# Key matmul before V's in the woven projections, and the norm of the attention's output in two parts

## The chip, the cores and the metric

The program runs on 8 cores of one Trainium2 chip (cores 0 to 3 on one die, 4 to 7 on the other) with no exchange between them. Each core has five engines with a queue of its own: TensorE (PE; weight loads stand as PEld), VectorE (DVE), ScalarE (ACT), GpSimd (POOL) and SyncE (SP), which here only issues DMAs. An engine works through its queue in order and stops where it waits for a semaphore. The metric is the device time of the slowest core, in us, as the median of several runs.

## The reference, cut to what matters

Each core has one batch element b = core // 2 and every second block of 128 of its rows: 2048 tokens of its own, and keys and values of all 4096. Sizes: D 1024, 16 heads, a latent of 128, 32 channels a head for scores, 32 for values, and an FFN of 4096 inner channels.

```python
q = rms_norm((x @ Wq).reshape(b, t, 16, 64).transpose(0, 2, 1, 3))
kv = x @ Wkv                                  # t x 128
k = rms_norm((kv @ Wk)...)                    # 16 heads x 32
v = (kv @ Wv)...                              # 16 heads x 32
probs = softmax(causal(q[..., :32] @ k.T / 8))
x1 = layernorm(x + pad(probs @ v) @ Wo)       # post-norm
gate, up = silu(bitlinear(x1, w_gate)), bitlinear(x1, w_up)
y = layernorm(x1 + bitlinear(gate * up, w_down))
# bitlinear: activations scaled by the row's maximum to -128..127 and rounded,
# weights scaled by their mean absolute value and rounded to -1, 0, 1
```

## The kernel before

The program is recorded once: helpers `pe`, `act`, `dve`, `pool` and `dma` append an instruction to an engine's queue, with the semaphore values (cT, cA, cV, cG for TensorE, ScalarE, VectorE, GpSimd) that it waits for. So the order in a queue is the order in which the Python code runs, and that is woven from generators: whoever calls `next` on one of them appends its next piece.

**Attention** (`attention`, L810). The core's 2048 queries are four groups `tc` of 512; in each, four groups `gi` of four heads; in each, the key blocks `sc` of 128 (8 tc + 8 of them): 320 steps. One step puts four score matmuls (L827) into four PSUM banks, two exponentials of 128x1024 on ScalarE (L840), a mask on GpSimd for diagonal blocks (L848 or L853), and, two steps late (LAG 2), the sums of probabilities into `ps_den` (L782) and the products with V into `ps_pv` (L793). After the last block of a group of heads `chain` (L763) empties both banks and divides, on VectorE (L771 to L776). After a `tc` its four tiles of 128 rows are appended to `wo_pend`, the list of pieces of `wo_ln1`.

**Pieces woven into the steps.** (1) While there are any left, one stage of `projections` (L617) follows each step. (2) From the fourth block of a group of heads on, `wo_step(2)` takes two pieces of `wo_pend`, unless the FFN is in its down projection. (3) Pieces of the weight stream (`stream_step`): per FFN weight block an absolute sum (DVE L366 or ScalarE), or two casts (DVE L382 and L385, 1.3 to 1.4 us each), with loads and stores. (4) Once projections and stream are done, the FFN (`ffn`, L1161) is woven in at a fixed rate: `up` (matmuls L986; ScalarE L999; VectorE L1005, L1017, L1022), quantization of the hidden rows (GpSimd L1058, VectorE L1061, a DMA transpose), `down` (L1109), and its own norm. A unit u is two tiles (2u, 2u+1); `down` first waits, by its yields, until `wo_pend` is empty (or the attention is over).

**Projections.** Chunks of 512 tokens, c5 = 2 to 7 in this woven part: for even c5 four jobs `queries2` (three stages), for each c5 four jobs `keys_values2` (two stages and a last piece), and `latent2` (L528), 8 matmuls in two halves, which makes the latent of the next chunk, second to last of the jobs of each. A key/value job (L563) makes V (matmul L567, VectorE's copy into `vtok` L571), the keys (matmul L575), their squares (ScalarE L432), in the next stage `inv_rms` (matmul L441 with ones, ScalarE Ln L448 and Exp L451), and at its end VectorE's product `khat` (L582). All of it shares two PSUM banks, `ps_w0` and `ps_w1`, from a ring `wring` that hands out the bank that was given back first:

```python
b3 = wring.take()          # V's bank: matmul L567, copy L571, then given back
b1 = wring.take()          # key's bank: matmul L575, held until khat (L582)
```

The loop around the jobs keeps one job `old` whose last piece is outstanding:

```python
for _ in range(stages):
    next(job)
    if old is not None:
        next(old, None)
        old = None
    yield
old = job
```

**Norm of the attention's output** (`wo_ln1`, L704). For tile `ti` (buffer `r_t[ti % 2]`, named r_t or S in the trace): `project(0)` and `project(1)` (four matmuls with Wo each, L714, and VectorE's add of x, L719), `norm1` (`layernorm_stats`: two bn_stats L690 and bn_aggr L692 on VectorE, then two tiny operations on GpSimd, L693 and L696, the second of which makes the power -0.5; then VectorE's normalization L727 of 128x1024), `quant` (VectorE L731, L733, L734, L735, L736, L738), and `store` (two stores and the load of x of tile ti + 2; it also sets `ln_done`, on which the FFN's `try_prologue` goes). `store` has an empty piece ahead of it, so a tile is six pieces, three steps. Two places finish `wo_pend` at once: `chain` of the next `tc`'s first group of heads (gi == 0), and the end of the attention. `factors` (L939, VectorE L942 to L946) needs `swb`, the mean of the FFN's weights (L336).

## Time and profile before

| | us |
|---|---|
| runs of the kernel before: median of 3 (each) | 1638.44 (1638.44, 1637.69, 1682.19) |
| the profiled execution, its own time | 1643.48 |
| its span on the slowest core (6); the other cores | 1641.9; 1625.1 to 1640.1 |
| mean granted TensorE clock, share of 2.4 GHz | 0.851 to 0.858 over the cores |
| busy on that core: TensorE, VectorE, ScalarE, GpSimd | 1302.4, 806.2, 824.7, 317.9 |

By stretches of the slowest core (busy us and granted clock):

| us | what runs | TensorE | DVE | ACT | clock |
|---|---|---|---|---|---|
| 0 to 90 | first projections, loads of x and weights | 34.9 | 23.4 | 37.6 | 0.80 |
| 90 to 205 | attention tc 0 (to 218), woven projections | 80.5 | 72.6 | 78.5 | 0.70 |
| 205 to 300 | tc 1 (218 to 475), projections, norms of tiles 0 to 3 | 62.0 | 56.6 | 55.7 | 0.71 |
| 300 to 455 | tc 1, projections | 120.3 | 88.9 | 120.7 | 0.50 and 0.69 |
| 455 to 560 | tc 2, norms of tiles 4 to 7, the FFN starts | 74.5 | 67.8 | 67.0 | 0.69 |
| 560 to 1190 | tc 2 and 3 with FFN woven in | 547.0 | 263.1 | 421.3 | 0.94 |
| 1190 to 1642 | norms of tiles 12 to 15, rest of the FFN | 383.3 | 233.8 | 44.0 | 0.93 |

How to read it: no engine is busy throughout, TensorE comes nearest; what each stretch is worth is told by the waits in it. In a timeline a row is start, duration, engine, line, operation, out<-in with shapes, and in brackets how long the engine had been idle before it and for whom. "x4" counts instructions that the row puts together.

### The profile page before, as it was taken

What the parts mean: (1) busy time and instruction counts of PE and PEld (TensorE: products, weight loads), DVE (VectorE), ACT (ScalarE), POOL (GpSimd) and SP (SyncE); (2) the same over time, 40 slices, a digit from 0 to 9 for tenths busy, and PEclk for the clock granted to TensorE, in tenths of its full rate; (3) what the DMA queues carried; (4) which work ended last, traced back from release to release, by engine and by line L of the source; (5) the groups of instructions that cost most, each with busy time, mean ns of one, the idle gap of its engine ahead of it and who ended that gap; (6) DMA issues with size and microseconds to landing.
All of it is one profiled execution on the core that took longest, in us unless ns stands there. A gap on an engine that the chain in (4) does not pass through costs nothing.

```text
span 1641.9 us, 22928 instructions; the slowest of 8 cores (1625.1 to 1641.9 us)
## 1 busy us (share of the span) xinstructions
PE 1302.4 (79%) x7494; PEld 438.3 (27%) x7494; DVE 806.2 (49%) x1158; ACT 824.7 (50%) x998; POOL 317.9 (19%) x350
## 2 busy tenths in 40 slices
PE   1676675788666888979869898989868999898966
PEld 0221121122111222222212222222223444343422
DVE  2227875468447766143561434143347762635522
ACT  2577564878784676657546686768601210111100
POOL 1024412033020304121123003130220020202021
PEclk8876686567556998989979998999989999898978
DMA  9995765779595785523255232523165585765646
GB/s 249 275 274 168 224 213 192 172 250 276 188 272 191 259 231 157 130 80 101 85 159 130 90 91 73 159 81 105 60 179 197 176 209 189 169 206 155 187 138 159
DMA packets 146514, 283.07 MB, mean 172 GB/s; under 512 B 91744, under 2 KB 92000, under 8 KB 133088
## 3 DMA queue, kind: packets, MB, share of 16 engines
q1 hardware_dynamic: 144816, 272.70, 54.6%
q0 software_dynamic: 1584, 8.91, 3.5%
q8 instruction: 64, 1.05, 0.3%
q14 instruction: 50, 0.41, 0.1%
HBM read 235.96 MB, written 33.55 MB: 164 GB/s over the span
## 4 chain that ended last, share of the span: by engine, by line
PE 51%; DVE 18%; issue 11%; ACT 8%; DMA 7%; POOL 3%; SPq 1%; DVEq 1%; ACTq 0%; POOLq 0%
PE ps_w L986 14%; PE ps_w L1109 6%; PE ps_sc L827 6%; ACT PT L840 5%; PE ps_den L782 4%; PE ps_sc L986 4%; PE ps_pv L793 3%; PE ps_sc L1109 3%; DVE S L775 3%; DMA R<-scr_w 2%; PE ps_w L547 2%; DVE st L690 2%; DMA R<-R 2%; DVE qb L382 2%; PE ps_w L714 2%
## 5 line engine op out<-in xcount | busy, mean ns | idle before, releaser
L840 ACT ACTIVATE PT<-ps_sc,negM 128x1024 bf16<-128x1024 f32 (+3 forms) x640 | 592.7, 983 | 197.6 <-PE ps_sc L827 195.3
L986 PE MATMUL ps_w<-R,S 128*128 128x512 fp8e4 x1280 | 336.1, 393 | 34.0 <-DVE R L1005 20.3
L827 PE MATMUL ps_sc<-qn,khat 32*128 32x512 bf16 (+3 forms) x1280 | 200.4, 397 | 63.5 <-ACT PT L840 58.7
L848 POOL TENSOR_TENSOR PT<-PT,tri 128x512 bf16<-128x512 bf16 x64 | 80.3, 1254 | 530.4 <-ACT PT L840 528.7
L986 PEld LDWEIGHTS ps_w<-R,S 128*128 128x128 bf16 x1280 | 106.4, 99 | 210.2 <-issue 121.0
L782 PE MATMUL ps_den<-PT,ones 128*32 128x512 bf16 (+3 forms) x1280 | 131.7, 402 | 18.4 <-DVE S L771 10.3
L853 POOL TENSOR_SCALAR PT<-PT,hflag_sb 128x512 bf16<-128x512 bf16 x64 | 112.9, 1763 | 111.0 <-ACT PT L840 110.9
L793 PE MATMUL ps_pv<-PT,vtok 128*32 128x512 bf16 (+3 forms) x1280 | 130.6, 398 | 0.1
L1109 PE MATMUL ps_w<-R 128*128 128x512 fp8e4 x416 | 114.2, 401 | 14.1 <-DMA R<-R 11.2
L986 PE MATMUL ps_sc<-R,S 128*128 128x512 fp8e4 x512 | 116.3, 386 | 8.8 <-DMA R<-scr_w 8.7
L1005 DVE SCALAR_TENSOR_TENSOR R<-R,ps_w 128x512 f32<-128x512 f32 x80 | 54.8, 685 | 137.2 <-ACT R L999 137.2
L827 PEld LDWEIGHTS ps_sc<-qn,khat 32*128 32x128 bf16 x1280 | 52.7, 93 | 255.0 <-issue 251.2
L999 ACT ACTIVATE R<-ps_sc,xsT 128x512 f32<-128x512 f32 x32 | 22.0, 687 | 186.9 <-PE ps_sc L986 158.1
L999 ACT ACTIVATE R<-ps_w,xsT 128x512 f32<-128x512 f32 x80 | 55.0, 687 | 97.5 <-PE ps_w L986 80.4
L1109 PE MATMUL ps_sc<-R 128*128 128x512 fp8e4 x320 | 75.3, 396 | 25.3 <-DMA R<-R 25.3
L1058 POOL TENSOR_SCALAR R<-R,fs 128x512 f32<-128x512 f32 x96 | 67.5, 714 | 107.8 <-DVE R L1061 68.6
L693 POOL TENSOR_SCALAR mv<-mv 128x1 f32<-128x1 f32 x32 | 7.1, 223 | 416.2 <-DVE mv L692 416.0
L1061 DVE TENSOR_SCALAR R<-R 128x512 bf16<-128x512 f32 x128 | 57.6, 491 | 55.5 <-DMA R<-R 34.5
L1017 DVE TENSOR_TENSOR R<-R,ps_w 128x512 f32<-128x512 f32 x72 | 49.4, 686 | 61.4 <-PE ps_w L986 59.7
L432 ACT ACTIVATE S<-ps_w 128x512 bf16<-128x512 f32 x48 | 28.7, 597 | 87.2 <-PE ps_w L575 56.1
L385 DVE TENSOR_SCALAR qb<-qb 128x2048 fp8e4<-128x2048 int8 x48 | 67.2, 1401 | 8.7 <-DVE qb L382 8.1
L1022 DVE TENSOR_REDUCE am<-R 128x1 f32<-128x512 f32 x96 | 65.9, 686 | 9.9
(182 smaller groups left out, 1379.2 us busy)
## 6 DMA issues: line engine op xcount, KB each, us to landing
R<-scr_w SPq DMA_DIRECT2D x192, 512.0 KB, 4.5
R<-wffn SPq DMA_DIRECT2D x69, 1024.0 KB, 7.6
scr_w<-qb SPq DMA_DIRECT2D x48, 256.0 KB, 6.6
khat<-wffn SPq DMA_DIRECT2D x9, 1024.0 KB, 15.0
vtok<-wffn SPq DMA_DIRECT2D x9, 1024.0 KB, 7.8
R<-xt POOLq DMA_DIRECT2D x7, 1024.0 KB, 13.7
R<-scr_x SPq DMA_DIRECT2D x12, 512.0 KB, 5.8
y<-R SPq DMA_DIRECT2D x12, 512.0 KB, 7.4
```

What stands on the lines that cost most here:

```text
L385: t2 = st["fi"] = dve(lambda e, o=o: e.tensor_scalar(fq[o], fi, 1.0, None, ALU.min, saturate=False), [t, t_fq[o]])
L782: pe(lambda e, j=j: e.matmul(ps_den[32 * j:32 * j + 32, stc:512], ones32[:], PT[pp][:, j * 512 + stc:j * 512 + 512], start=(sc == 0), stop ...
L793: t = pe(lambda e, j=j, h=h: e.matmul(ps_pv[32 * j:32 * j + 32, stc:512], vtok[:, h:h + 32], PT[pp][:, j * 512 + stc:j * 512 + 512], start ...
L827: t = pe(lambda e, j=j, gi=gi, tc=tc, kc=kc, stc=stc: e.matmul(ps_sc[:, j * 512 + stc:j * 512 + 512], khat[32 * j:32 * j + 32, kc:kc + 128 ...
L840: t = act(lambda e, hf=hf, pp=pp, stc=stc: e.activation(PTr[pp][:, 2 * hf:2 * hf + 2, stc:512], PSr[:, 2 * hf:2 * hf + 2, stc:512], AF.Exp ...
L848: t = pool(lambda e, pp=pp, stc=stc: e.tensor_tensor(PTr[pp][:, :, stc:stc + 128], PTr[pp][:, :, stc:stc + 128], tri.rearrange("p (r n) -> ...
L853: t = pool(lambda e, pp=pp, stc=stc: e.tensor_scalar(PTr[pp][:, :, stc:stc + 128], PTr[pp][:, :, stc:stc + 128], hflag[:, 0:1], None, ALU. ...
L986: t = pe(lambda e, c=c, b=b, kw=kk[w], i=i: e.matmul(wring.bufs[b], xqT[u % 2][:, i * 1024 + c * 128:i * 1024 + c * 128 + 128], wbuf[kw][: ...
L999: tt = act(lambda e, k=k, b=b, ti=ti: e.activation(tg[k], wring.bufs[b], AF.Tanh, scale=xsT[:, ti:ti + 1]), [t, t_xs[u], tg_free[k]])
L1022: t_am.append(dve(lambda e: e.tensor_reduce(am[:, p + 8 * i + io:p + 8 * i + io + 1], hh, AX, ALU.max, apply_absolute_value=True), [t3]))
L1058: t1 = pool(lambda e, cs=cs, hh=hh: e.tensor_scalar(hm[hh], hs.h[i][:, cs:cs + 512], fs[:, p + 6 + i:p + 7 + i], MAGIC, ALU.mult, ALU.add) ...
L1109: t = pe(lambda e, c=c, ic=ic, b=b, kw=kw, i=i: e.matmul(wring.bufs[b], hs.hqT[i][:, ic * 128:ic * 128 + 128], wbuf[kw][:, c * 512:(c + 1) ...
```

## The change

Three edits. In `keys_values2` the key matmul and its squares are recorded ahead of V's matmul and copy, with the bank taken first. In the loop of the jobs the old job's last piece (`khat` or `qn`) is recorded ahead of the next job's stage instead of behind it. In `wo_ln1` `norm1` and `quant` are cut otherwise: `stats` (bn_stats, bn_aggr, the two GpSimd operations), an empty piece, `norm1_quant` (L727 and the whole quantization), an empty piece, `store`, an empty piece: eight pieces, four steps a tile. No arithmetic changes.

```diff
         def keys_values2(c5, hc):
             kb = kvT[c5 % 2]
+            b1 = wring.take()
+            p1 = wring.bufs[b1]
+            t1 = pe(lambda e: e.matmul(
+                p1, wk[:, hc * 128:(hc + 1) * 128], kb, start=True, stop=True),
+                [t_kv[c5], wring.free[b1]], True)
+            t_sq = squares([(t1, p1)])
             b3 = wring.take()
             p3 = wring.bufs[b3]
-            t3 = pe(lambda e: e.matmul(
+            t3 = t_last[c5] = pe(lambda e: e.matmul(
                 p3, kb[:, hc * 128:(hc + 1) * 128], wv, start=True, stop=True),
-                [t_kv[c5], wring.free[b3]], True)
+                [wring.free[b3]], True)
...
             wring.give(b3, ends["v"])
-            b1 = wring.take()
-            p1 = wring.bufs[b1]
-            t1 = t_last[c5] = pe(lambda e: e.matmul(
-                p1, wk[:, hc * 128:(hc + 1) * 128], kb, start=True, stop=True),
-                [wring.free[b1]], True)
-            t_sq = squares([(t1, p1)])
             yield
...
                 for _ in range(stages):
-                    next(job)
                     if old is not None:
                         next(old, None)
                         old = None
+                    next(job)
                     yield
...
-            def norm1():
-                t_rs = layernorm_stats([state[0], state[1]], 0)
+            def stats():
+                state["rs"] = layernorm_stats([state[0], state[1]], 0)
+
+            def norm1_quant():
                 state["n"] = dve(lambda e: e.tensor_scalar(
-                    rt, rt, mv[:, 0:1], mv[:, 2:3], ALU.subtract, ALU.mult), [t_rs])
-
-            def quant():
+                    rt, rt, mv[:, 0:1], mv[:, 2:3], ALU.subtract, ALU.mult), [state["rs"]])
...
-            return [lambda: project(0), lambda: project(1), norm1, quant, None, store]
+            return [lambda: project(0), lambda: project(1), stats, None, norm1_quant, None, store,
+                    None]
```

In the changed file the key matmul is L567, V's L573, its copy L577, the normalization L729, and lines from some L655 on stand one lower (L828 for L827, and so on).

**Where the key/value jobs meet.** TensorE's queue in the woven projections, two key/value jobs one behind the other. L441 is the old job's matmul with ones, L827 scores, L782 and L793 the attention's sums and products with V. Before:

```order
L441 MATMUL ps_w1<-S,bd32 128x512
L827 MATMUL ps_sc<-qn,khat 128x512 x2
L782 MATMUL ps_den<-PT1,ones32 32x128 x4
L827 MATMUL ps_sc<-qn,khat 128x512 x2
L793 MATMUL ps_pv<-PT1,vtok 32x128 x4
L567 MATMUL ps_w1<-R 128x512
L575 MATMUL ps_w1<-R 128x512
L827 MATMUL ps_sc<-qn,khat 128x512 x2
```

and with the change:

```order
L441 MATMUL ps_w1<-S,bd32 128x512
L828 MATMUL ps_sc<-qn,khat 128x512 x2
L783 MATMUL ps_den<-PT1,ones32 32x128 x4
L828 MATMUL ps_sc<-qn,khat 128x512 x2
L794 MATMUL ps_pv<-PT1,vtok 32x128 x4
L567 MATMUL ps_w0<-R 128x512
L573 MATMUL ps_w1<-R 128x512
L828 MATMUL ps_sc<-qn,khat 128x512 x2
```

The two matmuls of the new job change places and no longer share a bank: the key matmul (now L567) takes the bank in which the old job's keys stood until `khat`, V's (L573) the one that the old job's L441 left when ScalarE had read it (Ln). Nineteen of the 24 jobs read like this.

The other five stand between the halves of a `latent2` (L528) before:

```order
L528 MATMUL ps_w1<-R 128x512 x4
L827 MATMUL ps_sc<-qn,khat 128x256 x2
L782 MATMUL ps_den<-PT0,ones32 32x384 x4
L827 MATMUL ps_sc<-qn,khat 128x256 x2
L793 MATMUL ps_pv<-PT0,vtok 32x384 x4
L567 MATMUL ps_w0<-R 128x512
L575 MATMUL ps_w0<-R 128x512
L528 MATMUL ps_w1<-R 128x512 x4
L827 MATMUL ps_sc<-qn,khat 128x128 x2
```

and with the change:

```order
L528 MATMUL ps_w0<-R 128x512 x4
L828 MATMUL ps_sc<-qn,khat 128x256 x2
L783 MATMUL ps_den<-PT0,ones32 32x384 x4
L828 MATMUL ps_sc<-qn,khat 128x256 x2
L794 MATMUL ps_pv<-PT0,vtok 32x384 x4
L528 MATMUL ps_w0<-R 128x512 x4
L567 MATMUL ps_w1<-R 128x512
L573 MATMUL ps_w0<-R 128x512
L828 MATMUL ps_sc<-qn,khat 128x128 x2
```

The latent's second half is recorded first; the key matmul then takes the bank that is free already, and V's, behind it, the bank that the latent's copy leaves.

**The norm of tile 3.** VectorE's queue from the second add of Wo's projection (L719) to the chain of the next group of queries (L771 to L776). Before:

```order
L690 BN_STATS st<-r_t 128x6 x2
L692 BN_AGGR mv<-st 128x2
L727 TENSOR_SCALAR r_t<-r_t,mv 128x1024
L731 TENSOR_REDUCE sm<-r_t 128x1
L733 TENSOR_SCALAR xsA<-sm 128x1
L734 RECIPROCAL sm<-xsA 128x1
L735 TENSOR_SCALAR sm<-sm 128x1
L736 TENSOR_SCALAR S<-r_t,sm 128x1024
L738 TENSOR_SCALAR S<-S 128x1024
L571 CAST vtok<-ps_w 128x512
L582 TENSOR_TENSOR khat<-ps_w,S 128x512
L571 CAST vtok<-ps_w 128x512
```

(behind these come L582, an absolute sum L366 and the chain, L771). With the change, ending with the chain's first rows:

```order
L366 TENSOR_REDUCE wabs<-khat 128x1
L690 BN_STATS st<-r_t 128x6 x2
L692 BN_AGGR mv<-st 128x2
L729 TENSOR_SCALAR r_t<-r_t,mv 128x1024
L731 TENSOR_REDUCE sm<-r_t 128x1
L733 TENSOR_SCALAR xsA<-sm 128x1
L734 RECIPROCAL sm<-xsA 128x1
L735 TENSOR_SCALAR sm<-sm 128x1
L736 TENSOR_SCALAR S<-r_t,sm 128x1024
L738 TENSOR_SCALAR S<-S 128x1024
L772 TENSOR_SCALAR S<-ps_den 128x512
L774 COPY pvb<-ps_pv 128x512
```

The adds and the statistics stand some five rows later, and the normalization and quantization of this tile are put right ahead of the chain, since the steps up to it are too few for four tiles of four steps; no copy or `khat` stands between them.

**Where the FFN starts.** VectorE's queue around the norm of tile 6; L382 and L385 are casts of the weight stream, L1169 and L942 to L946 the FFN's factors, L1005 its first product. Before:

```order
L690 BN_STATS st<-S 128x6 x2
L692 BN_AGGR mv<-st 128x2
L727 TENSOR_SCALAR S<-S,mv 128x1024
L731 TENSOR_REDUCE sm<-S 128x1
L733 TENSOR_SCALAR xsA<-sm 128x1
L734 RECIPROCAL sm<-xsA 128x1
L735 TENSOR_SCALAR sm<-sm 128x1
L736 TENSOR_SCALAR S<-S,sm 128x1024
L738 TENSOR_SCALAR S<-S 128x1024
L382 TENSOR_SCALAR qb<-R,wscl 128x2048
L385 TENSOR_SCALAR qb<-qb 128x2048
L1169 SCALAR_TENSOR_TENSOR swgu<-swb 128x1
```

and with the change (L1170 and L943 to L947 are the factors here):

```order
L385 TENSOR_SCALAR qb<-qb 128x2048
L1170 SCALAR_TENSOR_TENSOR swgu<-swb 128x1
L943 TENSOR_SCALAR xsC<-xsA 128x2
L944 TENSOR_SCALAR xsT<-xsC,swb 128x2
L946 TENSOR_TENSOR xsC<-xsC 128x2
L947 TENSOR_SCALAR xsC<-xsC,swgu 128x2
L690 BN_STATS st<-S 128x6 x2
L692 BN_AGGR mv<-st 128x2
L1006 SCALAR_TENSOR_TENSOR R<-R,ps_w 128x512
L382 TENSOR_SCALAR qb<-R,wscl 128x2048
L385 TENSOR_SCALAR qb<-qb 128x2048
L729 TENSOR_SCALAR S<-S,mv 128x1024
```

The factors stood behind the whole norm of tile 6 and a pair of casts; now they stand ahead of its statistics, and the normalization follows after the first product (L1006).

**The end of the attention.** Since `down` is begun only when `wo_pend` is empty, four steps more of it in tiles 8 to 11 leave 16 matmuls of the up projection (L986, L987 in the changed file) to stand behind the attention's last L793, between the projections with Wo of tile 12. Before, L1109 of the down projection stood there.

## Rows read from the trace of the kernel before

**Rows 1.** Busy time by stretch: start:end, span, then busy (count) per engine, clock, DMA, GB/s.

```profile
300.00:355.00 55.00, 43.64 (x190) 10.46 (x191) 27.10 (x28) 41.78 (x51) 10.50 (x7) 0.50 0.76 208
455.00:560.00 105.00, 74.45 (x432) 20.56 (x431) 67.82 (x91) 67.03 (x75) 20.82 (x20) 0.69 0.74 235
835.00:1180.00 345.00, 304.63 (x2114) 90.49 (x2111) 121.85 (x194) 236.87 (x256) 62.74 (x69) 0.94 0.37 109
```

**Rows 2.** Waits from 90 to 560 us: who waited for whom, total, times, longest.

```profile
PE ps_w L575 <- DVE vtok L571: 47.3, 21, 8.8
ACT S L432 <- PE ps_w L575: 56.1, 20, 8.8
PE ps_w L567 <- DVE khat L582: 15.7, 5, 5.8
```

**Rows 3.** Timeline (start, us, engine, line, [wait]): first and last of 15 short L575 waits.

```profile
145.31 0.58 PE L575 MATMUL ps_w<-R 128*128 128x512 bf16 x1 [0.94 <-DVE vtok L571]
...
449.51 0.58 PE L575 MATMUL ps_w<-R 128*128 128x512 bf16 x1 [0.94 <-DVE vtok L571]
```

**Rows 4.** Timeline 177 to 182 us, one hand-over between two key/value jobs.

```profile
177.65 0.63 ACT L451 ACTIVATE S<-S 128x512 f32<-128x512 f32 x1
178.19 0.61 PE L567 MATMUL ps_w<-R 128*128 128x512 bf16 x1
178.90 0.69 DVE L571 CAST vtok<-ps_w 128x512 bf16<-128x512 f32 x1 [0.47 <-PE ps_w L567]
179.74 0.58 PE L575 MATMUL ps_w<-R 128*128 128x512 bf16 x1 [0.94 <-DVE vtok L571]
180.42 0.60 ACT L432 ACTIVATE S<-ps_w 128x512 bf16<-128x512 f32 x1
```

**Rows 5.** Timeline, waits behind the norms of tiles 1, 2 and 3.

```profile
237.73 3.40 PE L714 MATMUL ps_w<-S 128*128 128x512 bf16 x8 [2.00 <-DVE qn L559]
...
269.11 0.59 PE L575 MATMUL ps_w<-R 128*128 128x512 bf16 x1 [6.36 <-DVE vtok L571]
...
278.84 1.28 DVE L690 BATCH_NORM_STATS2 st<-r_t 128x6 f32<-128x512 f32 x2
282.94 0.81 DVE L727 TENSOR_SCALAR r_t<-r_t,mv 128x1024 f32<-128x1024 f32 x1 [2.51 <-POOL mv L696]
286.89 0.69 DVE L738 TENSOR_SCALAR S<-S 128x1024 bf16<-128x1024 f32 x1 [0.17 <-DVE S L736]
288.33 0.58 PE L575 MATMUL ps_w<-R 128*128 128x512 bf16 x1 [8.80 <-DVE vtok L571]
```

**Rows 6.** Timeline 505 to 541 us, the start of the FFN.

```profile
505.91 1.02 PE L714 MATMUL ps_w<-S 128*128 128x512 bf16 x4 [2.05 <-DVE swb L336]
...
515.32 0.81 DVE L727 TENSOR_SCALAR S<-S,mv 128x1024 f32<-128x1024 f32 x1 [1.20 <-POOL mv L696]
519.89 1.28 DVE L382 TENSOR_SCALAR qb<-R,wscl 128x2048 int8<-128x2048 f32 x1
524.21 1.28 ACT L999 ACT_TABLE_LOAD   x1 [8.52 <-DVE xsC L946]
527.13 1.87 PE L714 MATMUL ps_w<-S 128*128 128x512 bf16 x4 [10.95 <-DVE R L1005]
...
540.85 0.59 PE L986 MATMUL ps_w<-R,S 128*128 128x512 fp8e4 x1 [5.35 <-DVE R L1017]
```

**Rows 7.** Timeline 1183 to 1245 us, the end of the attention.

```profile
1184.49 1.15 POOL L848 TENSOR_TENSOR PT<-PT,tri 128x512 bf16<-128x512 bf16 x1
1190.42 1.97 POOL L853 TENSOR_SCALAR PT<-PT,hflag_sb 128x512 bf16<-128x512 bf16 x1
1192.54 0.30 PE L782 MATMUL ps_den<-PT,ones 128*32 128x128 bf16 x4 [6.45 <-POOL PT L853]
1200.21 1.91 PE L1109 MATMUL ps_sc<-R 128*128 128x512 fp8e4 x4
1207.19 1.22 DVE L727 TENSOR_SCALAR S<-S,mv 128x1024 f32<-128x1024 f32 x1 [1.21 <-POOL mv L696]
```

## Prediction

> **What bounds the kernel now.** I read the busy time by stretch first. From 835 to 1180 us the attention has FFN matmuls woven in, and TensorE is busy 305 of 345 us at a granted clock of 0.94 [rows 1]: little of this change's kind of wait is left there. In the stretches that hold the woven projections and the norms of tiles 0 to 7 no engine is full: 43.6 of 55 us on TensorE at clock 0.50 (the 1.2 GHz level throughout), and 74 of 105 us at 0.69 [rows 1]. There time goes in waits, so I read the waits from 90 to 560 us next. TensorE waits 47.3 us in 21 waits for VectorE's copy of V (L571) before the key matmul L575, and ScalarE then waits 56.1 us in 20 waits for L575 before its Square (L432) [rows 2]. ScalarE makes all exponentials of the attention, so an idle ScalarE there is lost time, unless TensorE is later still.
>
> The 21 waits are of two kinds. Fifteen are of 0.94 to 1.58 us [rows 3], some 15.0 us together: V's matmul, then its copy, then the key matmul in the same PSUM bank. The other six sum to 47.3 - 15.0 = 32.3 us: VectorE reached the copy late because something long stood before it. The longest, 8.80 us, stands behind tile 3's norm: bn_stats at 278.84, a gap in which VectorE waited 2.51 us for GpSimd's power, the normalization at 282.94, the quantization to 287.58, and only then the copy, so that the key matmul starts at 288.33 [rows 5].
>
> **Part 1, key matmul first (with the old job finished first).** No instruction is added or removed. Where a latent projection has just been woven in (5 of the 24 jobs), the order shows the key matmul with no wait of its own and V's waiting for an older khat: there a short wait goes whole, about 1.1 us each, 5.6 us. In the other jobs the key matmul takes the bank that the old job's khat product frees, so it waits for L582 now. At one hand-over ScalarE's Exp ends at 178.28; khat could run about 178.4 to 179.1, the key matmul from 179.25 and Square from about 179.9 instead of 180.42 [rows 4]. So ScalarE gains some 0.5 us where it was idle, TensorE nothing: before, V's matmul (0.61) and the 0.94 wait lay beside that Exp, and V's 0.61 now stands behind the key matmul [rows 4]. Ten such jobs at 0.35 us (some were not idle) give 3.5. Sum of part 1: -9 us. Bounds: -15.0, if every short wait goes [rows 3], and +11, if the 19 jobs that now wait for khat each put V's 0.6 us before the scores with nothing won. I stay nearer the first since the five latent cases are certain by the order. The long waits do not shorten: the khat product stands in the slot on VectorE in which V's copy stood, so a chain or a cast before it delays the key matmul as before; also the 15.7 us of waits for khat that are there already [rows 2] stay.
>
> **Part 2, the norm in two parts.** bn_stats and the two small GpSimd operations go one step ahead of the normalization and quantization. Two things are removed: VectorE's wait of 1.20 us for GpSimd per tile [rows 6], and about 1.5 us of statistics from the front of each train; what is left, L727 to L738, is 282.94 to 287.58, 4.6 us, in one piece as before [rows 5]. I count only where something waits.
>
> *Tiles 0 to 3.* For tile 1 the q product moves ahead of the train, and the projection of Wo that waited 2.00 us for it [rows 5] is free: -2. For tiles 2 and 3 the copies stood behind the whole train (6.36 us for tile 2, 8.80 for tile 3 [rows 5]). Now a key matmul after tile 2 waits for a khat behind a 4.6 us train, some 4 us, and after each projection of Wo about 2 us for the two adds. Tile 3's last parts no longer fit in the first group of heads and are flushed ahead of its closing chain, as the order shows: statistics 1.3 + 0.2, the 1.2 wait and the 4.6 train then delay the release of ps_den, of which two attention steps hide part; I take 5 us on TensorE. Together 15.2 becomes 11: -4. Sum -6; bounds -17 (all of it goes) and +4 (nothing of 15.2 goes beyond the 2, and the flush costs 6).
>
> *Tiles 4 to 7, where the FFN starts.* Here TensorE waits 10.95 us for L1005, behind tile 6's norm, a quantized weight (1.28 for the first of its two casts), the factors and a table load of 1.28, and then 5.35 us for L1017 behind tile 7's norm [rows 6]. In the new order the factors stand ahead of tile 6's statistics and train: by then VectorE has done less by two GpSimd waits (2.4), one pair of statistics (1.5) and one train (4.6), 8.5 us, and the statistics run while ScalarE loads its table. The second wait loses statistics, one 1.2 us wait and some of the adds, 3 us. Tile 7's train then stands alone between two later FFN products and makes a new wait, 4 us; the weight scale gets ahead of tile 5's train, and 2.05 us of wait for it go [rows 6]. 8.5 + 3 + 2 - 4 = 9.5; I take -9. Bounds: -14 (no new wait) and -3 (a train of 4.6 and two casts land in the new one).
>
> *FFN against attention.* Eight list entries a tile instead of six make four steps more for four tiles. During tiles 8 to 11 the down projection waits for the last, so 16 FFN matmuls come after the attention instead of in it. They cost from 2.3 us (0.144 each, the mean in the woven stretch [rows 1]) to 7.6 (0.48 each in rows 7's first four of L1109), less what the attention's steps shorten by: +2, bounds 0 and +7.6.
>
> *End of the attention.* The last diagonal mask, L853, could start at 1185.64, when L848 ends, but GpSimd first works at the FFN's quantization and starts it at 1190.42, for 1.97 us; TensorE waits 6.45 us [rows 7]. With the up projection not finished by then, nothing stands before it: -4.8. In exchange that quantization is exposed behind the last 16 up matmuls; before, TensorE began L1109 at 1200.21 with two parts already transposed [rows 7]. Scales, GpSimd, VectorE and a transpose take some 8 us of which matmuls of Wo hide little; but the down projection was starved by them before as well: +4, bounds 0 and +10. Sum -1.
>
> **The sum.** -9 - 6 - 9 + 2 - 1 = -23 us. The profiled execution took 1643.5 us, so 1620.5; it lies 5.0 us over the median of 1638.4, so I predict 1616 as a median. A measurement of this kernel can tell about 2%, 33 us, from no change.
>
> One rule speaks against splitting. The row: L727 takes 0.81 us alone [rows 5] and 1.22 beside GpSimd's L1058 [rows 7], 0.4 more; GpSimd's two norm operations now run beside VectorE's casts in tiles 1, 2, 5 and 6, so at most 4 x 0.4 = 1.6 us of the 23 is lost. The Trainium skill (SBUF — State Buffer, "Who interferes with whom") says that the two engines share a pair of ports as an exclusive lock held for a whole instruction; by that, a cast could hold GpSimd up for its 1.3 us, which delays nothing here, since the power is wanted a step later, and the sum would stand.
>
> **Rivals.**
> *A, waits only change hands (0.27).* Every key matmul waits as long for khat as it did for V's copy, the flush before the chain eats what tiles 2 and 3 give, and only the start of the FFN gains. For it: 19 of 24 jobs do wait for khat by the order, and Exp ends only 0.09 us before the old V matmul began or after it [rows 4]. Against it: ScalarE's 56.1 us [rows 2]. Time: -9 + 2 - 1 = -8, 1630.
>
> *B, slower (0.10).* One mechanism: khat's product needs ScalarE's Exp, which stands behind exponentials and behind the absolute sums of the weight stream. If Exp is late in every one of the 19 jobs, TensorE waits in order with the next scores behind it, and ScalarE then starves. It decides from about 1.3 us more per job (19 x 1.3 = 25, against 23 won); at 2 us it is 38 - 23 = +15, 1653. Against it: in rows 4 Exp is in time.
>
> *C, the clock comes back (0.15).* In the woven stretches TensorE runs at 0.50 and 0.69 of its clock, between waits, and at 0.94 where it hardly waits [rows 1]. If shorter waits lift the 0.69 to 0.85 over the 105 us of the FFN's start, its 74.5 busy us become 60.5, 14 less, half of it on the path; the same in the 55 us at 0.50 gives 43.6 to about 31, again half: 7 + 6 = 13 more, 1603. The Trainium skill (TensorE: Matmul & The Clock Gate, "HAM oscillation — how this bites in real kernels") says that idle gaps between bursts put the array back to half rate; the trace agrees so far as 0.50 stands where the waits are densest.
>
> **The numbers.** The forecast (0.48) covers 1607 to 1627. With A (to 1642), C (down to 1596) and B beyond, 1600 to 1643 leaves out about 0.2. Faster by over 2% (under 1605.7): most of C and a little of the forecast, 0.17. Slower by over 2% (over 1671): the far end of B, 0.03. Within 2%: 0.80.
>
> **What would show it.** Part 1: the waits of the key matmul (now L567) fall well under 47, name khat, and ScalarE's waits for it fall from 56 to about 40. Part 2: no VectorE wait on the power beyond a few; the 10.95 wait at the FFN's start is under 3; a wait of ps_den of about 5 us near 300. End: L853 right behind L848, and a gap of some 8 us before L1109. The prediction is wrong if the key matmul's waits for khat sum to 40 or more, or if TensorE's busy time moves by over 15 us through the clock.

## The result: slower by 1.9%, and the profile with the change

The changed kernel took 1681.79 us as a median of its runs, the kernel before 1641.42 beside it; the ratio is 1.019, with a 95% interval of 1.0147 to 1.0233. (The medians hold some runs in which one die ran at a lower clock; every ratio here leaves those out and is what to go by, and the three runs of the change without it took 1669.73, 1670.35, the profiled one, and 1673.91 us.) I had predicted 1616, a gain of 1.4%: the sign is wrong, and the time lies outside the range.

Where the time went is read first from one event that both kernels have in the same places: VectorE empties `ps_den` at the end of each group of heads. Core 3 of both is used for this, on which the first such event stands at 123.0 us before and at 124.9 with the change. Timeline of VectorE before, the last group of tc 1, the last of tc 2, the first of tc 3 and the last of all:

```profile
476.77 0.69 DVE L771 TENSOR_SCALAR S<-ps_den 128x512 f32<-128x512 f32 x1 [6.99 <-PE ps_pv L793]
...
789.65 0.69 DVE L771 TENSOR_SCALAR S<-ps_den 128x512 f32<-128x512 f32 x1 [2.81 <-PE ps_pv L793]
...
913.58 0.68 DVE L771 TENSOR_SCALAR S<-ps_den 128x512 f32<-128x512 f32 x1
...
1193.54 0.69 DVE L771 TENSOR_SCALAR S<-ps_den 128x512 f32<-128x512 f32 x1 [2.01 <-PE ps_pv L793]
```

and with the change:

```profile
505.34 0.69 DVE L772 TENSOR_SCALAR S<-ps_den 128x512 f32<-128x512 f32 x1 [8.99 <-PE ps_pv L794]
...
813.77 0.69 DVE L772 TENSOR_SCALAR S<-ps_den 128x512 f32<-128x512 f32 x1 [2.81 <-PE ps_pv L794]
...
917.30 0.69 DVE L772 TENSOR_SCALAR S<-ps_den 128x512 f32<-128x512 f32 x1 [13.96 <-PE ps_pv L794]
...
1194.83 0.69 DVE L772 TENSOR_SCALAR S<-ps_den 128x512 f32<-128x512 f32 x1 [2.23 <-PE ps_pv L794]
```

The stretch of the woven projections ends 28.6 us later (505.34 against 476.77). The rest of tc 2 is 4.4 shorter (308.4 against 312.9), the first group of heads of tc 3 20.4 shorter (103.5 against 123.9), the next three 2.4 shorter, and the tail behind the attention 18.5 longer (the spans of core 3 are 1632.9 and 1652.7). So there are two things to explain: a loss of 28.6 us, and a shift of some 20 us from tc 3 into the tail.

Core 3 alone understates the loss. The woven projections begin ahead of that first event, and as a mean of the eight cores of the two profiled executions it comes 7.0 us later with the change (120.4 and 127.4). From there to the end of tc 1 it is 28.3 us more (353.1 and 381.4), and behind tc 1 10.2 less; the mean span grows by 25.0 (1633.7 and 1658.7).

Who waited for whom in the woven projections, TensorE on core 3, with the change (before, the rows that answer are [rows 2], and core 3 has 47.9 for the copy of V, 15.1 for `khat` and 4.1 for `khat` ahead of a query matmul):

```profile
PE ps_w L567 <- DVE khat L582: 40.8, 16, 6.3
...
PE ps_w L528 <- DVE khat L582: 21.6, 5, 11.2
PE ps_w L547 <- DVE qn L559: 21.0, 9, 5.5
PE ps_w L567 <- DVE qn L559: 6.3, 3, 3.2
PE ps_w L547 <- DVE khat L582: 4.1, 2, 2.7
```

The key matmul's waits (L567) came to 40.8 + 6.3 = 47.1 us, where V's and the key matmul's had been 63.0. That part went as the change meant it. But two lines are new: the latents (L528) wait 21.6 us for `khat` and the query matmuls (L547) 21.0 for `qn`. Together they are 42.6 us where 0.7 us stood. 42.6 - 0.7 and 47.1 - 63.0 make +26.0, and V's matmul (L573) waits 2.5 us more for the latent's copy, against the 28.6 us by which the stretch grew.

The longest of these waits, 11.22 us, comes from two of the edits together. Timeline with the change, core 3:

```profile
318.96 0.68 DVE L772 TENSOR_SCALAR S<-ps_den 128x512 f32<-128x512 f32 x1
...
324.22 0.68 DVE L582 TENSOR_TENSOR khat<-ps_w,S 128x512 bf16<-128x512 f32 x1
325.05 1.86 PE L528 MATMUL ps_w<-R 128*128 128x512 bf16 x4 [11.22 <-DVE khat L582]
```

The latent waits for a `khat` that stands on VectorE behind tile 3's whole norm, put ahead of the chain, and behind the chain too. With the norm as before (`x1_proj`, below) the longest wait of a latent is 6.2 us.

One of these waits close up. Before, core 6, a query job's second stage ends and the next query job's first matmuls follow:

```profile
105.11 0.63 ACT L451 ACTIVATE S<-S 128x512 f32<-128x512 f32 x1
105.16 1.89 PE L547 MATMUL ps_w<-R 128*128 128x512 bf16 x8
...
105.84 0.75 DVE L559 SCALAR_TENSOR_TENSOR qn<-ps_w,gq,S 128x512 bf16<-128x512 f32 x1 [3.78 <-ACT S L451]
```

and with the change, core 0:

```profile
103.03 0.63 ACT L451 ACTIVATE S<-S 128x512 f32<-128x512 f32 x1
...
103.77 0.75 DVE L559 SCALAR_TENSOR_TENSOR qn<-ps_w,gq,S 128x512 bf16<-128x512 f32 x1 [7.07 <-ACT S L451]
104.66 3.06 PE L547 MATMUL ps_w<-R 128*128 128x512 bf16 x8 [1.59 <-DVE qn L559]
```

Before, the eight query matmuls (L547) ran beside ScalarE's Exp (L451). With the change they begin only behind `qn`: 1.59 us of wait. And they take 3.06 us instead of 1.89. Windows around them, with the change (core 0: ahead of the wait's end, and the matmuls):

```profile
96.00:104.60 8.60, 6.14 (x47) 2.11 (x46) 1.45 (x2) 8.29 (x12) 2.73 (x2) 1.00 0.99 327
104.60:107.70 3.10, 3.04 (x10) 0.97 (x10) 0.00 (x0) 0.22 (x1) 1.15 (x1) 0.60 1.06 337
```

and before (core 6):

```profile
105.10:107.00 1.90, 1.88 (x14) 0.73 (x10) 0.75 (x1) 1.78 (x3) 1.09 (x1) 1.00 1.04 362
```

The granted clock is 1.00 up to the gap and 0.60 behind it, so part of it is at the lower of its two levels of 1.2 and 2.4 GHz; before it is 1.00 over the same eight matmuls. Here the wait costs more than its own length. The 1.59 us are not the only difference: in the 8.60 us up to these matmuls TensorE is busy 6.14 us with the change and 8.37 before (96.50 to 105.10, core 6). And over the whole stretch the clock adds little: from the first event to the end of tc 1 TensorE's matmuls are busy 246.3 us before, 251.5 with the change and 246.6 in `x1_proj` (means of eight cores), while its waits are 105.8, 129.7 and 136.2 us.

The reason is in the ring, and there my description ahead of the prediction was wrong. I wrote that `wring` hands out the bank that was given back first. Its code goes by turns and skips only a bank that is held:

```python
def take(self):
    for _ in self.bufs:
        k = self.i % len(self.bufs)
        self.i += 1
        if not self.held[k]:
            self.held[k] = True
            return k
```

Before, the next job took its bank while the old job still held its own. The held bank was skipped, and the job got the one that ScalarE's Ln had left long before. With the old job's last piece recorded first, nothing is held, and the turn falls on the bank that `khat` or `qn` has just been told to read. Jobs of every kind, not the key/value jobs alone, then wait for VectorE. And VectorE waits for ScalarE: in the rows with the change above Exp ends at 103.66 and `qn` starts at 103.77. That the cost lies in the bank, and not in the order as such, is shown by experiments 3, 4 and 6 below.

The places of the norms: the wait of 10.95 us for L1005 [rows 6] is gone, and at the end of the attention TensorE waits 0.79 us for the mask L854 where it was 6.45 [rows 7]. But behind it stands a new wait. Timeline with the change, core 0:

```profile
1208.63 0.24 PE L783 MATMUL ps_den<-PT,ones 128*32 128x128 bf16 x4 [0.79 <-POOL PT L854]
...
1224.65 1.37 POOL L1059 TENSOR_SCALAR R<-R,fs 128x512 f32<-128x512 f32 x2 [16.17 <-DVE fs L1051]
...
1229.95 3.57 PE L1110 MATMUL ps_den<-R 128*128 128x512 fp8e4 x8 [8.40 <-DMA R<-R]
...
1243.93 2.30 PE L1110 MATMUL ps_den<-R 128*128 128x512 fp8e4 x8 [3.76 <-DMA R<-R]
...
1254.05 1.89 PE L1110 MATMUL ps_den<-R 128*128 128x512 fp8e4 x8 [3.95 <-DMA R<-R]
```

GpSimd begins the quantization of unit 3 at 1224.65, and the down projection then waits for each transposed part, 8.40, 3.76 and 3.95 us. Before, L1109 began at 1200.21 [rows 7].

### The profile page after: what moved, and what is told of

The parts are those of the page before. It is cut to its first block, busy times and chain, and to the rows that moved or that the text cites. A ratio compares the mean times of both kernels' runs of the same rounds, so it can differ in the third digit from the quotient of the medians.

```text
span 1668.8 us, 22904 instructions; the slowest of 8 cores (1649.6 to 1668.8 us)
## 1 busy us (share of the span) xinstructions
PE 1318.6 (79%) x7494; PEld 441.9 (26%) x7494; DVE 805.3 (48%) x1158; ACT 825.9 (49%) x998; POOL 319.4 (19%) x350
## 4 chain that ended last, share of the span: by engine, by line
PE 55%; DVE 15%; issue 11%; ACT 9%; DMA 6%; POOL 2%; SPq 1%; DVEq 0%; ACTq 0%; POOLq 0%
PE ps_w L987 14%; PE ps_w L1110 7%; PE ps_sc L828 6%; ACT PT L841 5%; PE ps_sc L987 5%; PE ps_den L783 4%; PE ps_sc L1110 4%; PE ps_w L547 3%; DVE S L776 3%; PE ps_pv L794 3%; DMA R<-scr_w 2%; DMA R<-R 2%; DVE qb L382 2%; PE ps_w L714 2%; DVE st L690 1%
## 5 line engine op out<-in xcount | busy, mean ns | idle before, releaser
L987 PE MATMUL ps_w<-R,S 128*128 128x512 fp8e4 x1256 | 337.5, 399 | 49.9 <-DVE R L1006 19.3
L828 PE MATMUL ps_sc<-qn,khat 32*128 32x512 bf16 (+3 forms) x1280 | 204.0, 399 | 64.0 <-ACT PT L841 59.6
L987 PEld LDWEIGHTS ps_w<-R,S 128*128 128x128 bf16 x1256 | 105.6, 100 | 229.1 <-issue 146.4
L854 POOL TENSOR_SCALAR PT<-PT,hflag_sb 128x512 bf16<-128x512 bf16 x64 | 111.9, 1748 | 110.4 <-ACT PT L841 110.4
L794 PE MATMUL ps_pv<-PT,vtok 128*32 128x512 bf16 (+3 forms) x1280 | 129.8, 396 | 0.0
L987 PE MATMUL ps_sc<-R,S 128*128 128x512 fp8e4 x528 | 120.4, 385 | 7.6 <-DMA R<-scr_w 7.5
L828 PEld LDWEIGHTS ps_sc<-qn,khat 32*128 32x128 bf16 x1280 | 53.5, 93 | 262.8 <-issue 258.5
L1006 DVE SCALAR_TENSOR_TENSOR R<-R,ps_w 128x512 f32<-128x512 f32 x79 | 54.1, 685 | 141.2 <-ACT R L1000 141.2
L1110 PE MATMUL ps_w<-R 128*128 128x512 fp8e4 x384 | 104.7, 397 | 13.0 <-DMA R<-R 12.8
L547 PE MATMUL ps_w<-R 128*128 128x512 bf16 x192 | 66.1, 507 | 25.8 <-DVE qn L559 20.4
L1018 DVE TENSOR_TENSOR R<-R,ps_w 128x512 f32<-128x512 f32 x71 | 48.7, 686 | 59.0 <-PE ps_w L987 56.2
L987 PEld LDWEIGHTS ps_sc<-R,S 128*128 128x128 bf16 x528 | 52.2, 99 | 72.6 <-issue 12.4
```

Of the source, the lines that this page charges most:

```text
L547: t1 = pe(lambda e, c=c, cc=cc, p1=p1: e.matmul(p1, wq[:, c * D + cc:c * D + cc + 128], x[:, c * 512:(c + 1) * 512], start=(c == 0), stop= ...
L794: t = pe(lambda e, j=j, h=h: e.matmul(ps_pv[32 * j:32 * j + 32, stc:512], vtok[:, h:h + 32], PT[pp][:, j * 512 + stc:j * 512 + 512], start ...
L828: t = pe(lambda e, j=j, gi=gi, tc=tc, kc=kc, stc=stc: e.matmul(ps_sc[:, j * 512 + stc:j * 512 + 512], khat[32 * j:32 * j + 32, kc:kc + 128 ...
L854: t = pool(lambda e, pp=pp, stc=stc: e.tensor_scalar(PTr[pp][:, :, stc:stc + 128], PTr[pp][:, :, stc:stc + 128], hflag[:, 0:1], None, ALU. ...
L987: t = pe(lambda e, c=c, b=b, kw=kk[w], i=i: e.matmul(wring.bufs[b], xqT[u % 2][:, i * 1024 + c * 128:i * 1024 + c * 128 + 128], wbuf[kw][: ...
L1110: t = pe(lambda e, c=c, ic=ic, b=b, kw=kw, i=i: e.matmul(wring.bufs[b], hs.hqT[i][:, ic * 128:ic * 128 + 128], wbuf[kw][:, c * 512:(c + 1) ...
```

## The experiments

All start from the kernel before. Which of the three edits loses the time? The theory that I formed from the two traces, "turns of the ring", says: the old job's last piece first, and that alone. Its rivals: the key matmul first, or the norm in two parts.

**1. The projections' part alone** (`x1_proj`): both edits of the projections, the norm as before.

> Only the projections' part of the change (key matmul first, old job's last piece first); the norm is as before. The trace of the whole change puts 28 us of the loss into the stretch of the woven projections (on core 3 the last chain before the second group's norms starts at 476.8 us before and at 505.3 with the change). Theory T (turns of the ring): the old job's last piece, recorded first, gives its bank back, and the ring's turn then hands out just that bank, so that every next job waits for khat or qn. Expected: about 1668 us (1660 to 1680), ratio 1.017, and TensorE waits for khat and qn of 80 to 95 us in the woven part. Rival N (the norm in two parts is to blame for the loss, its trains now standing before khat): about 1640 us here, ratio 1.00.

Measured: 1.0233 (1.0188 to 1.0278). The loss is in the projections, and it is above the 1.017 that was expected. TensorE's waits on core 3 name the same lines as in the whole change, with 21.6 us for `qn` and 16.6 at the latents; all its waits for `khat` and `qn` in these jobs come to 99.6 us, over the 80 to 95 expected.

**2. The norm's part alone** (`x2_norm`): split, eight pieces a tile.

> Only the norm in two parts with eight pieces a tile; the projections are as before. Theory T: behind the projections the trace of the change is 9 us shorter than before on core 3 (a start of the FFN 5 shorter, the first group of heads of the last 512 queries 20 shorter, the tail behind the attention 18 longer), so about 1632 us (1622 to 1640), ratio 0.994. Rival N: the norm's parts are to blame, 1660 us or more, ratio 1.012 or more. My prediction's sum for this part was -14 without the projections, 1627.

Measured: 0.9939 (0.9915 to 0.9964), a gain of 10 us, as the theory said from the later stretches. The two halves multiply to 1.017, the whole change measured 1.019.

**3. The old job first, V's matmul still ahead** (`x3_old`):

```diff
                 for _ in range(stages):
-                    next(job)
                     if old is not None:
                         next(old, None)
                         old = None
+                    next(job)
                     yield
```

> Only the old job's last piece recorded first; V's matmul still stands ahead of the key matmul, and the norm is as before. Theory T: all of the loss is in this edit, about 1670 us (1660 to 1682), ratio 1.018, V's matmul now waiting for khat. Rival K (it is the key matmul put first, into the bank of the old keys, that costs): about 1641 us, ratio 1.00.

Measured: 1.0222 (1.0169 to 1.0276). It is the whole loss of `x1_proj`, without the key matmul being moved. The rival that blames the key matmul falls. TensorE's waits, core 3 (L567 is V's matmul here):

```profile
PE ps_w L567 <- DVE khat L582: 41.1, 15, 9.3
PE ps_w L547 <- DVE qn L559: 22.2, 9, 5.5
```

**4. The same order, another bank** (`x7_bank`): `x1_proj`, and the ring of two avoids the bank just given back.

```diff
             k = self.i % len(self.bufs)
-            self.i += 1
+            if len(self.bufs) == 2 and self.given == k and not self.held[1 - k]:
+                k = 1 - k
+            self.i = k + 1
...
         self.free[k] = tok
+        self.given = k
```

> The whole edit of the projections (as in the first of these), but of two banks that are both given back the ring hands out the one given back longer ago: the key matmul, a query job or a latent takes the bank that ScalarE's Ln has left, and V's matmul the one that khat leaves. Recorded order the same. Theory T: the loss goes, and the short waits of the key matmul for V's copy go as well: about 1630 us (1620 to 1641), ratio 0.994. Rival O (the order in VectorE's queue, khat ahead of the copy, costs, whichever the bank): about 1668 us, ratio 1.017.

Measured: 0.9896 (0.9865 to 0.9926). Same instructions, and VectorE's queue in the same order as in `x1_proj`; only the banks differ, and 1.0233 becomes 0.9896, some 55 us. The order of VectorE's queue is not what costs. TensorE's waits, core 3:

```profile
PE ps_w L577 <- DVE khat L586: 34.9, 12, 8.8
...
PE ps_w L577 <- DVE qn L563: 13.1, 3, 6.5
...
PE ps_w L577 <- DVE R L538: 2.2, 3, 0.7
...
PE ps_w L551 <- DVE qn L563: 1.8, 1, 1.8
```

(L577 is V's matmul here, L551 a query matmul, L586 `khat`.) No latent waits for `khat`, and query matmuls wait 1.8 us. The hand-over that was [rows 4] now reads, core 3:

```profile
177.11 0.63 ACT L455 ACTIVATE S<-S 128x512 f32<-128x512 f32 x1
...
177.64 0.61 PE L571 MATMUL ps_w<-R 128*128 128x512 bf16 x1
...
178.07 0.68 DVE L586 TENSOR_TENSOR khat<-ps_w,S 128x512 bf16<-128x512 f32 x1
178.90 0.59 PE L577 MATMUL ps_w<-R 128*128 128x512 bf16 x1 [0.65 <-DVE khat L586]
```

From the first of the two matmuls to the end of the second it is 1.85 us, and it was 2.13 [rows 4]: the wait for `khat` is 0.65 where the wait for the copy was 0.94.

**5. Is it the key matmul's being first that gains there?** (`x9_vbank`): `x3_old` with the ring of `x7_bank`. V's matmul takes Ln's bank, the key matmul that of `khat`.

> As x7_bank (old job's last piece first, older bank first), but V's matmul stands ahead of the key matmul: V takes the bank that Ln has left, the key matmul the one that khat leaves. Theory K (what x7_bank gained, it gained by giving ScalarE its squares without any wait for VectorE): about 1641 us, ratio 0.998 to 1.004, since the key matmul waits for khat now, some 48 us in the woven part. Rival P (what counts is that the two matmuls no longer share one bank, whichever is first): about 1627, ratio 0.990.

Measured: 0.9896 (0.9868 to 0.9923), the same as `x7_bank`. My theory K falls: the order of the two matmuls makes no difference. What both have and the kernel before has not is two banks for V's and the key matmul. Both also record `khat` ahead of V's copy, and the one can't be had here without the other: while the old job holds one of two banks, only one is left. So that the separate banks bring the 1.0% is likely and not shown apart. ScalarE's waits in the two, core 3, first `x7_bank`:

```profile
ACT PT L844 <- PE ps_sc L831: 48.7, 24, 6.7
ACT S L436 <- PE ps_w L551: 23.5, 17, 3.3
ACT S L452 <- PE ps_w L445: 9.2, 10, 6.0
ACT S L436 <- PE ps_w L571: 8.0, 6, 2.2
```

and `x9_vbank`:

```profile
ACT S L436 <- PE ps_w L579: 53.0, 17, 8.8
ACT S L436 <- PE ps_w L551: 22.8, 17, 3.5
ACT S L452 <- PE ps_w L445: 8.5, 9, 6.0
ACT PT L844 <- PE ps_sc L831: 8.4, 8, 2.2
```

The key matmul first takes ScalarE's wait for it from 53.0 to 8.0 us (L436 is the Square), and gives it back as waits for scores, 48.7 instead of 8.4. The sums are 89.4 and 92.7. TensorE has one gap either way, and ScalarE meets it one instruction later.

The Trainium skill (Perfetto Trace Analysis, "Matmuls") says that independent matmul groups should rotate through different PSUM banks, so that one's eviction overlaps the next one's matmuls. These two runs agree with it, by 1.0% together with the earlier `khat`, for two matmuls that had shared a bank. `x3_old` shows its limit: there too the two matmuls stand in different banks, and it is 2.2% slower, since the turn gives out the bank that is still being read.

**6. Which jobs pay?** The older bank for query jobs and latents alone (`x12_qfix`), and for key/value jobs alone (`x13_kfix`), both in `x1_proj`:

```diff
+                    wring.older = job.__name__ != "keys_values2"   # == in x13_kfix
                     next(job)
+                    wring.older = False
```

> The projections' part of the change with the older of the two banks for the query jobs and the latents alone; the key/value jobs take their banks as in the change (key matmul in the bank that khat leaves, V's in Ln's). Norm as before. In the trace of x1_proj TensorE waits 44 us for khat and qn ahead of query and latent matmuls, 5 before; ahead of the key/value matmuls it is 55 us, and 62 before (for the copy and khat). Theory M (all of the loss sits in the query jobs and latents, which my prediction left out): ratio 0.992 (0.988 to 1.000), about 1630 us. Rival J (it sits in the key/value jobs): 1.012 or more, 1660 us.

Measured: 0.9932 (0.9906 to 0.9958).

> The reverse: the older bank for the key/value jobs alone, query jobs and latents as in the change. Norm as before. Theory M: ratio 1.020 (1.012 to 1.025), about 1675 us. Rival J: 1.000 or less, 1642 us.

Measured: 1.0198 (1.0178 to 1.0218). The theory said 0.992 and 1.020. TensorE's waits in `x13_kfix`, core 3:

```profile
PE ps_w L578 <- DVE khat L587: 34.7, 12, 8.8
...
PE ps_w L552 <- DVE qn L564: 21.9, 9, 5.5
PE ps_w L533 <- DVE khat L587: 16.9, 5, 6.2
PE ps_w L578 <- DVE qn L564: 10.1, 3, 7.0
PE ps_w L552 <- DVE khat L587: 4.1, 2, 2.7
```

(L552 a query matmul, L533 a latent.) The loss stays where the lines L552 and L533 stay. With the query jobs and latents mended, the change's own banks for the key/value jobs gain 0.7% and the older banks 1.0%; the intervals of the two overlap, but `x1_proj` and `x13_kfix` differ by the same 0.35%.

The 0.7% has another source than I would have looked for. From the first event of `ps_den` to the end of tc 1, means of the eight cores of each profiled execution:

| us | stretch | TensorE's waits | its matmuls busy | clock |
|---|---|---|---|---|
| before | 353.1 | 105.8 | 246.3 | 0.64 |
| `x12_qfix` | 342.5 | 104.4 | 237.2 | 0.67 |
| `x7_bank` | 334.6 | 92.4 | 241.3 | 0.66 |
| `x9_vbank` | 335.2 | 93.9 | 239.9 | 0.67 |

In `x12_qfix` TensorE waits hardly less than before. Its matmuls, the same number, are busy 9.1 us less at a higher granted clock, and that is nearly all of the 10.6 us. In the two with the older bank the waits fell by 12 to 13 us and the busy time by 5 to 6. Why the clock is higher was not tried apart.

**7. V's matmul half a step later** (`x10_mid`): in `x7_bank` V's matmul and copy are recorded behind the next step's scores and sums, so that `khat` is done when its turn comes.

```diff
+            mid.append(values)       # V's matmul and copy
             yield
+            flush_mid()
...
+                        flush_mid()  # attention(): ahead of pv_mms
                         if old:
                             pv_mms(*old[1])
```

> x7_bank, with V's matmul and copy recorded half a step later, behind the next step's scores and sums and ahead of its products with V. In x7_bank V's matmul waits some 48 us for khat in the woven part and holds up the scores behind it. Theory W (those waits are lost time on TensorE): they fall under 10 us and the time to about 1600 us (1590 to 1615), ratio 0.975. Rival E (ScalarE's exponentials bound these steps, TensorE only waits elsewhere): about 1627, ratio 0.990, with waits of TensorE for exponentials in their place.

Measured: 0.9925 (0.9902 to 0.9947), no better than `x7_bank`, rather worse. Neither theory had it right: V's waits fell, to 19.4 + 4.8 = 24.2 us, but not under 10, and a wait that I had called small took their place. TensorE, core 3:

```profile
PE ps_w L445 <- DVE vtok L583: 23.9, 23, 3.3
PE ps_w L580 <- DVE khat L590: 19.4, 4, 7.7
PE ps_w L580 <- DVE qn L563: 4.8, 2, 2.8
```

The matmul with ones (L445) needs a bank too, and the only one free is V's: it waits 23 times for V's copy, some 1.0 us each. Its own sum of waits, taken as in the table above, is 98.1 us. With two banks for three users the wait moved from one to another.

**8. What of the norm's gain is the split, what the longer list?** `x4_len` is the kernel before with two empty pieces more a tile (`norm1, quant, None, store, None, None`). `x5_norm3` is the split with six pieces (`stats, None, norm1_quant, store`).

> The kernel before with two empty pieces more behind store: eight pieces, four steps a tile, but norm and quantization as before in one step; projections as before. It tells what of x2_norm's gain (0.9939) is the later pieces alone. Theory V (the gain is the shorter trains of VectorE and its spared waits for GpSimd): here none of it, ratio 1.000 (0.997 to 1.006). Rival F (the gain is the shift of the FFN's matmuls and of the tiles' norms by the two pieces more): ratio 0.994.

Measured: 1.0046 (1.0028 to 1.0064). The two pieces more cost half a per cent, so the split itself gains about one.

> The norm split in two parts one step apart, but with six pieces a tile (stats, an empty piece, norm with quantization, store): three steps a tile as before, projections as before. x2_norm gave 0.9939 with eight pieces, and eight pieces without a split 1.0046. Theory V (split and length add up): 0.989 (0.986 to 0.992), about 1625 us. Rival G (a store in the step of its norm holds SyncE's queue back, or the split lives from its longer spacing): 0.994 or more, 1633 us.

Measured: 0.9929 (0.9909 to 0.995). It is nearer to `x2_norm`'s 0.9939 than to the 0.989 that the sum of parts would give; the intervals of the two overlap, and 0.989 lies outside. So the length's cost isn't simply got back. That the store's place in the norm's step costs something (rival G) wasn't tried apart.

Where the length costs is told by the stretches, means of the eight cores of each profiled execution:

| us | before | `x2_norm` | `x4_len` | `x5_norm3` |
|---|---|---|---|---|
| tc 1, first group of heads | 83.4 | 80.1 | 91.1 | 77.2 |
| tc 2, first group (the FFN starts) | 95.4 | 95.6 | 95.6 | 91.7 |
| tc 3, first group | 123.4 | 106.3 | 107.6 | 124.3 |
| behind the attention | 443.8 | 458.7 | 462.0 | 436.9 |
| tc 3 and all behind it | 847.6 | 841.7 | 846.7 | 842.5 |

The shift from tc 3 into the tail that the whole change shows (-20.4 and +18.5 on core 3) is the list's length: it comes in both kernels with eight pieces and not with six. Fewer FFN matmuls are woven in, and they and the quantization come behind the attention; the waits for transposed parts there rise on core 3 from 21.6 us before to 36.6 in `x4_len`. But the shift as a whole costs nothing: tc 3 and all behind it take 0.9 us less in `x4_len` than before.

Its loss is in the first group of heads of tc 1, 7.7 us. Core 3 of `x4_len`:

```profile
300.10 1.28 DVE L690 BATCH_NORM_STATS2 st<-r_t 128x6 f32<-128x512 f32 x2
...
308.31 0.62 PE L783 MATMUL ps_den<-PT,ones 128*32 128x512 bf16 x4 [2.25 <-DVE S L772]
```

Tile 3's norm, unsplit, no longer fits in and is put whole ahead of the chain (L772, at 307.48). The group's last products (L794) start at 303.40 here, 87.0 us behind the chain that opens the group; without the two pieces it was 82.9. Then the chain waits for the norm, and the next group for `ps_den`. The split pays for this: with as many pieces `x2_norm` takes 80.1 us there. So the length costs 7.7 us with the unsplit norm, and 2.9 with the split one (80.1 against 77.2). Split and length do not add up stretch by stretch.

**9. The whole change, mended** (`x8_both`: with the ring of `x7_bank`; `x11_three`: the same with `x5_norm3`'s list).

> The whole change with the mended choice of banks (of two banks the one given back longer ago). The two parts alone gave 0.9896 and 0.9939 of the time before. Theory T (they lie in different stretches and add up): 0.984, about 1617 us (1608 to 1625). Rival S (both live from the same slack of VectorE in the norms' stretches, so that khat now waits behind the trains): 0.990, about 1627.

Measured: 0.9833 (0.981 to 0.9856), median 1616.6 us. The parts add: 0.9896 x 0.9939 = 0.9836.

> x7_bank with that same norm (split, six pieces): the version that the experiments point to. Theory V: 0.9896 x 0.989 = 0.979, about 1608 us (1600 to 1614). Rival G: 0.983 as x8_both, 1616.

Measured: 0.9835 (0.9811 to 0.9859), median 1611.56 us. As `x5_norm3` foretold by then, six pieces give no more than eight. Both beat the kernel before by 1.7%. A gain of the size that the change was meant to bring is there; one choice of a bank turned it over.

## Why the prediction was wrong, point by point

**Part 1 (-9 us): the step that failed is the count of who is touched.** I priced the 24 key/value jobs, and for these the number was near: with the other jobs put right, the change's own banks gave 0.9932 (`x12_qfix`), -11 us, and my bounds were -15 and +11. That is luck in part. I had it come from short waits that go and an earlier Square, and TensorE's waits fell by 1.4 us only (105.8 to 104.4); the gain came as matmuls at a higher clock. But the edit of the loop moves the old job's last piece ahead of every job. The 12 query jobs and the latents stood in no term of the sum, neither in my 24 nor in the 19 of rival B: I had them at nothing. They cost 46.7 us of waits for `khat` and `qn` on TensorE (21.6 + 21.0 + 4.1) where there had been 4.8. The sum of part 1 was thus not -9 but about +38 (1.0233 of 1641). The sentence "no instruction is added or removed" was true and hid it: the waits hang on banks, and the piece of the order that I showed held only key/value jobs and halves of a latent. Even there one row told it: the latent's first half stood on another bank than before, and I gave no word to what it waits for. Of the five jobs beside a latent I wrote that V's matmul waits for an older `khat`; it waits for the latent's copy (L534), 2.5 us over four times on core 3.

**The mechanism that I took for the gain was not the one.** I argued from ScalarE's 56.1 us of waits for the key matmul [rows 2] that an earlier Square gains. `x7_bank` and `x9_vbank` show the same time with 8.0 and 53.0 us of that wait. The row named the instruction that happened to stand behind TensorE's gap. What both have less of is TensorE's own gaps in the ring's banks: 67.8 us before on core 3 (47.9 + 15.1 + 4.1 + 0.7), 52.0 in `x7_bank` (34.9 + 13.1 + 2.2 + 1.8), 50.1 in `x9_vbank` (33.8 + 13.1 + 2.7 + 0.5), and 0.65 instead of 0.94 at the hand-over shown. For `x12_qfix` this does not do: its gain is the clock's. With the change itself ScalarE's waits for the key matmul fell to 50.0 us on core 3, not to about 40.

**The size of a short wait.** "TensorE gains nothing" at the ten plain hand-overs: it gained 0.3 us in the one shown, so I was too careful there; and a wait for `khat` as long as that for the copy, rival A's picture, did not come.

**Part 2, tiles 0 to 3 (-6):** core 3 has 258.2 us from the end of tc 0 to that of tc 1 before, and 254.9 in `x2_norm`: -3.3, within my bounds. The flush ahead of the chain is there as I said: in the changed kernel `ps_den` is emptied right behind tile 3's L738, at 318.96. In `x2_norm` TensorE waits 2.26 us for `ps_den` behind it, not 5. With the whole change no wait for `ps_den` stands there at all; the flush comes out as the latent's 11.22 us, a path that my sum did not have.

**Part 2, the start of the FFN (-9):** the waits went, as worked out: no 10.2 us for L1005 and none for `swb` on core 3. The steps that failed are the size of the new waits, and the last one, from waits to time. Windows of core 3 from the last chain of tc 1 to the first of tc 2, before and `x2_norm`:

```profile
476.80:571.20 94.40, 68.56 (x423) 19.85 (x422) 69.47 (x97) 55.85 (x62) 16.50 (x16) 0.80 0.73 234
```

```profile
469.60:563.70 94.10, 73.96 (x423) 20.75 (x422) 69.59 (x96) 55.68 (x62) 18.32 (x16) 0.76 0.73 228
```

TensorE's waits for VectorE fell from 19.8 us (10.2 + 5.1 + 4.5) to 13.1 (9.7 for L1018, 2.4 and 1.0 for the adds), so by 6.7 and not by 9.5: the waits for L1018 rose from 5.1 to 9.7, where I had them fall by 3 with a new one of 4 beside. And the same 423 matmuls are busy 74.0 us instead of 68.6, at a granted clock of 0.76 instead of 0.80. On this core these 5.4 us took most of what was won. The clock's part is not steady over the cores: before, the eight have 0.76 to 0.80 in this stretch, in `x2_norm` 0.76 to 0.81. In the mean TensorE's waits fell by 2.0 us, its busy time rose by 2.0, and the stretch took 95.6 us instead of 95.4: the term of -9 came to nothing. With six pieces it took 91.7.

**FFN against attention (+2) and the end (-1):** both effects came, each far larger than its term, and nearly cancelled. tc 3's first group of heads gave 16 to 20 us over the three kernels with eight pieces, the tail took 16 to 21. Of the bounds 0 to +10 for the quantization behind the attention, DMA waits of +12 us on core 3 lie past the upper one. Together I had them at +1. From the start of tc 3 on, `x4_len` is 0.9 us shorter than before and `x2_norm` 5.9. What the longer list costs, 0.46% or 7.5 us in `x4_len`, lies in the first group of heads of tc 1, which I had not priced for the length. Two of my signs came: at the end of the attention the mask is in time, and L1110 then waits 8.40 us, where I had a gap of some 8.

**Part 2 as a whole:** -14 was forecast and -10 measured (`x2_norm`), and that is luck: the terms were -6, -9 and +1, and came to -3, 0 and -6.

**The rivals.** B was the case of the sign that came, with a chance of 0.10; its place was wrong (key/value jobs), and so was its size per job. Its mechanism is seen: VectorE waits 63.1 us for ScalarE's Exp ahead of `khat` and `qn` on core 3 (33.4 + 29.7), and 32.8 before. The waits that came new are in the latents and query jobs, 42.6 us over 14 waits named L528 or `qn`, 3.0 us each. The marks that I had set did their work: "wrong if the key matmul's waits for khat sum to 40 or more": they summed to 40.8 on core 3, though that wasn't where the time was lost. "VectorE's waits on the power": beyond a few they are gone, 2.4 + 3.1 us between 215 and 600 us on core 3, 9.8 + 6.1 before.

**The first prediction's sum, corrected:** projections +38, norm -10 (`x2_norm`), together +28, 1.017; the whole change measured 1.019. With the bank mended the sum is -17 - 10 = -27, and `x8_both` measured that, near my -23, but by other terms and for a kernel that the diff did not make.

## What to carry to other kernels

When an edit changes the order in which buffers are given back and taken, list for every user of the ring, not only for the edited one, which buffer it gets and whose last reader frees it. A gain priced at one user and a loss at the others come from the same line. A ring that goes by turns with few buffers should prefer the one given back longest ago. A wait line names who stands behind the gap: before pricing an engine's wait as gain, ask where the gap is met if that one instruction moves. And where work is woven in by steps, an empty piece in a list isn't free: it moves everything behind it, and what no longer fits is done at once at the next fixed point, here a whole norm ahead of a chain for which TensorE waited. Which of the moved stretches pays is read from all of them: the largest shift here, into the tail, cost nothing.
